# Re-ordered attention queues in a layer with split-precision matmuls: two score banks, three projection banks, work moved between VectorE, ACT and POOL

## The reference

```
x = x + attention(layernorm(x)) @ wo.T
    q, k, v = projections of layernorm(x); q = rope(q); k = rope(k)
    o[i] = sum over j <= i of exp(-slope_h * (i - j)) * (q[i] . k[j]) * v[j]
x = x + (fwht(silu(n @ W1.T) * (n @ W3.T))) @ W2.T      with n = layernorm(x)
```

## Time and profile before

| | us |
|---|---|
| median of 3 runs (range) | 283.77 (283.72 to 285.06) |
| the profiled execution | 284.03 |
| its span, first to last instruction | 282.2 |
| busy: PE / PEld / DVE / ACT / POOL | 260.7 / 225.8 / 222.1 / 162.2 / 132.6 |
| granted TensorE clock, mean | 1.000 |
| chain that ended last | PE 47%, DVE 37%, issue 7%, ACT 3%, DMA 2%, POOL 2% |

### The profile page before, as it was taken

One profiled execution on the slowest core, in us unless ns is written; L12 is line 12 of the kernel. 1 busy time (PEld: TensorE's weight loads), 2 busy tenths in 40 slices (PEclk: granted clock), 3 DMA queues, 4 the chain that ended last, 5 costly groups with the idle time before them and its releaser, 6 DMA issues.

```text
span 282.2 us, 4149 instructions
## 1 busy us (share of the span) xinstructions
PE 260.7 (92%) x1480; PEld 225.8 (80%) x1480; DVE 222.1 (79%) x340; ACT 162.2 (57%) x271; POOL 132.6 (47%) x101
## 2 busy tenths in 40 slices
PE   0798988999998899999999999889999999999995
PEld 0585877888786688878888888779889889988895
DVE  2878899999999998868999999999657795234323
ACT  1776877769377667655759657593643463033330
POOL 1049858477655746713584783478806500000000
PEclk9999999999999999999999999999999999999999
DMA  6694020220202110000001002200000000100002
GB/s 242 250 352 177 0 78 1 77 74 0 74 2 74 26 52 1 2 1 0 0 11 66 0 2 74 74 3 0 0 3 0 0 2 0 45 32 0 2 0 74
DMA packets 5203, 13.23 MB, mean 47 GB/s; under 512 B 576, under 2 KB 2112, under 8 KB 5184
## 3 DMA queue, kind: packets, MB, share of 16 engines
q1 hardware_dynamic: 4752, 12.65, 12.7%
q10 hardware_dynamic: 432, 0.33, 0.4%
HBM read 11.93 MB, written 1.05 MB: 46 GB/s over the span
## 4 chain that ended last, share of the span: by engine, by line
PE 47%; DVE 37%; issue 7%; ACT 3%; DMA 2%; POOL 2%; ACTq 0%; DVEq 0%
PE bank L263 16%; PE bank L264 15%; PE bank L265 15%; DVE rope_b L742 9%; DVE rope_a L741 6%; DVE bank L755 6%; DVE w_lo L716 5%; DVE o_lo L765 4%; DVE p_lo L760 4%; DMA sin_sb<-in_sin 2%; DVE xn L710 2%; PE bank L276 1%; POOL qk L625 1%; ACT o_hi L507 1%; DVE stats L693 1%
## 5 line engine op out<-in xcount | busy, mean ns | idle before, releaser
L625 POOL TENSOR_TENSOR qk<-rope_a,rope_b 128x512 f32<-128x512 f32 x40 | 52.1, 1304 | 54.8 <-DVE rope_b L742 54.8
L263 PE MATMUL bank<-xt_hi,w_hi 128*128 128x512 f32 x144 | 58.4, 405 | 3.4 <-DVE rope_a L741 2.3
L264 PE MATMUL bank<-xt_lo,w_hi 128*128 128x512 f32 x144 | 57.2, 397 | 0.0
L265 PE MATMUL bank<-xt_hi,w_lo 128*128 128x512 f32 x144 | 57.1, 396 | 0.0
L632 POOL TENSOR_TENSOR q_hid<-qk,q_hid 128x512 fp32r<-128x512 f32 x32 | 49.3, 1543 | 16.4 <-ACT q_hid L496 16.4
L503 ACT ACTIVATE p_hi<-bank 128x512 fp32r<-128x512 f32 x48 | 28.6, 597 | 40.5 <-DVE bank L755 40.1
L742 DVE TENSOR_TENSOR rope_b<-rope_b,sin_sb 128x512 f32<-128x512 f32 x40 | 43.3, 1083 | 0.0
L263 PEld LDWEIGHTS bank<-xt_hi,w_hi 128*128 128x128 f32 x144 | 27.6, 192 | 11.8 <-DVE rope_a L741 3.9
L265 PE MATMUL bank<-w_hi,o_lo 128*128 128x256 f32 x128 | 36.2, 283 | 0.0
L264 PE MATMUL bank<-w_lo,o_hi 128*128 128x256 f32 x128 | 36.2, 283 | 0.0
L263 PE MATMUL bank<-w_hi,o_hi 128*128 128x256 f32 x128 | 36.1, 282 | 0.0
(11 more groups left out here) (69 smaller groups left out, 574.0 us busy)
## 6 DMA issues: line engine op xcount, KB each, us to landing
w_raw<-in_w SPq DMA_DIRECT2D x6, 512.0 KB, 3.3
w_raw<-in_wq SPq DMA_DIRECT2D x4, 512.0 KB, 4.8
decay_sb<-in_decay SPq DMA_DIRECT2D x4, 512.0 KB, 5.6
w_raw<-in_wo SPq DMA_DIRECT2D x4, 512.0 KB, 3.3
x_sb<-in_x SPq DMA_DIRECT2D x4, 256.0 KB, 4.1
out<-x_sb SPq DMA_DIRECT2D x8, 128.0 KB, 1.8
w_raw<-in_wk SPq DMA_DIRECT2D x1, 512.0 KB, 5.7
w_raw<-in_wv SPq DMA_DIRECT2D x1, 512.0 KB, 7.4
```

The lines of the kernel that those rows point to most:

```text
L263: pe.matmul(o, a_hi, b_hi, start=first, stop=False, skip_group_check=shared)
L264: pe.matmul(o, a_hi, b_lo, start=False, stop=False, skip_group_check=shared)
L265: return pe.matmul(o, a_lo, b_hi, start=False, stop=last, skip_group_check=shared)
L625: pool.tensor_tensor(qk[:, r % 2, :], rope_a[:, r % 2, :], rope_b[:, r % 2, :], ALU.add).then_inc(rope_sum, 1)
```

## The change

- Projections use three banks in turn after the first eight tiles, scores two (banks 3 and 4): tile n = 3u + s takes bank n mod 2 and waits for the low part of tile n - 2. `p_hi` and `p_lo` get a second slot for `S_SECOND`, and ACT's `high_p` no longer waits for attention.
- PE's order in a unit: the key and the first query of unit u + 2 come before `S_FIRST1`, the second query behind it (before: both queries behind it and the key at the end).
- The orders of ACT, POOL and VectorE are rewritten to match. In unit 0 they are written out.
- The low parts of chunks 4 to 13 are written by POOL, those of 0 to 3 stay on VectorE; every wait for a chunk's low part names the engine's own semaphore through `wait_low_weights` (the SP loads, `project`, `project_values`, `project_out`, `up`). Chunk 3's parts come later, and chunk 4 is worked with the first ones (`FIRST_CHUNKS` 5), so each later chunk of the first half moves up by one unit.
- The norm of the halves prepared in units 0 to 5 and 8 to 13 is applied by ACT in unit 4 (12) as scale x + shift, with the shift computed by VectorE in unit 3 (11). The first half's and the feed-forward's last one stay on VectorE.

```diff
...
-FIRST_CHUNKS = 4
+FIRST_CHUNKS = 5
+LOW_ON_DVE = 4
...
-LIN = START + [i for u in range(UNITS) for i in values(u)[:2] + queries(u) + values(u)[2:] + key(u) + turned(u)]
+def projected(u):
+    return values(u)[:2] + key(u) + queries(u) + values(u)[2:] + turned(u)
+LIN = START + [i for u in range(UNITS) for i in projected(u)]
...
-FIRST_ROPE = 5
...
+LIN_BANKS, S_BANKS = 3, 2
+def p_slot(u, s):
+    return S_SECOND + 2 * (u % 2) if s == S_SECOND else s
...
-        p_hi = sb("p_hi", [P, 3, TOK], F32R)
-        p_lo = sb("p_lo", [P, 3, TOK], F32R)
+        p_hi = sb("p_hi", [P, 4, TOK], F32R)
+        p_lo = sb("p_lo", [P, 4, TOK], F32R)
...
+        shift = sb("shift", [P, TT])
...
-        s_bank = bank[2:5]
+        s_bank = bank[LIN_BANKS:LIN_BANKS + S_BANKS]
...
+        def wait_low_weights(engine, n):
+            if n < LOW_ON_DVE:
+                engine.wait_ge(w_lo_dve, n + 1)
+            else:
+                engine.wait_ge(w_lo_pool, n + 1 - LOW_ON_DVE)
...
-            return bank[n] if n < len(bank) else bank[n % 2]
+            return bank[n] if n < len(bank) else bank[(n - len(bank)) % LIN_BANKS]
+        def score_bank(u, s):
+            return s_bank[(3 * u + s) % S_BANKS]
...
                 if n >= len(bank):
-                    pe.wait_ge(lin_free, (n - 2 if n >= len(bank) + 2 else n - len(bank)) + 1)
+                    pe.wait_ge(lin_free, (n - LIN_BANKS if n >= len(bank) + LIN_BANKS else n - len(bank)) + 1)
                 return lin_bank(n)
...
-                if u:
-                    pe.wait_ge(p_lo_done, 3 * (u - 1) + s + 1)
+                n, o = 3 * u + s, score_bank(u, s)
+                if n >= S_BANKS:
+                    pe.wait_ge(p_lo_done, n - S_BANKS + 1)
...
-                        last = product(s_bank[s][:, b * 256:(b + 1) * 256], k_hi[:, ks, a], k_lo[:, ks, a],
+                        last = product(o[:, b * 256:(b + 1) * 256], k_hi[:, ks, a], k_lo[:, ks, a],
...
-                    last = product(s_bank[s][:], k_hi[:, ks, a], k_lo[:, ks, a],
+                    last = product(o[:], k_hi[:, ks, a], k_lo[:, ks, a],
...
                 if u < UNITS:
-                    fill(values(u)[:1])
+                    fill(values(u)[:2] + key(u) + queries(u)[:1])
                     scores(u, S_FIRST1)
-                    fill(values(u)[1:2] + queries(u))
+                    fill(queries(u)[1:] + values(u)[2:])
                 if u:
...
                 if u < UNITS:
-                    fill(values(u)[2:3])
                     attend(u, 0)
-                    fill(values(u)[3:] + key(u) + turned(u))
+                    fill(turned(u))
             up(0, 3)
...
+            def norm_apply(i, tiles):
+                half = i % HALVES
+                act.wait_ge(shift_done, i)
+                act.wait_ge(lin_full, LIN_NO[("X", i - 1, KD - 1)] + 1)
+                for t in tiles:
+                    act.activation(xn[:, t, :], x_sb[:, half * TT + t, :], ACT.Identity, bias=shift[:, t:t + 1],
+                                   scale=rstd[:, t:t + 1]).then_inc(xn_done, 1)
...
                 act.wait_ge(mask_done, n + 1)
-                if u:
-                    act.wait_ge(o_full, 2 * u - (s == S_FIRST0))
-                act.activation(p_hi[:, s, :], s_bank[s][:], ACT.Copy).then_inc(p_hi_done, 1)
+                act.activation(p_hi[:, p_slot(u, s), :], score_bank(u, s)[:], ACT.Copy).then_inc(p_hi_done, 1)
...
             high_weights(2)
-            high_weights(3)
             swap(("K", 0, 0))
             swap(("Q", 0, 0))
+            high_rope(("K", 0, 0))
             high_v(0, 0)
-            high_rope(("K", 0, 0))
             swap(("Q", 0, 1))
+            high_rope(("Q", 0, 0))
             high_v(0, 1)
-            high_rope(("Q", 0, 0))
             swap(("Q", 0, 2))
...
             high_v(0, 3)
+            high_weights(3)
+            high_weights(4)
+            high_p(0, S_FIRST0)
             high_rope(("Q", 0, 2))
-            high_p(0, S_FIRST0)
+            high_p(0, S_SECOND)
+            swap(("K", 0, 1))
+            high_p(0, S_FIRST1)
             high_rope(("Q", 0, 3))
-            high_p(0, S_SECOND)
-            for u in range(UNITS):
-                if u:
-                    before = queries(u - 1)
-                    fill(key(u - 1) + turned(u - 1))
-                    for item in before[:1]:
-                        high_rope(item)
-                    high_p(u, S_FIRST0)
-                    for item in before[1:]:
-                        high_rope(item)
-                    high_o(u - 1, 1)
-                    high_p(u, S_SECOND)
-                fill(values(u)[:2] + queries(u)[:1])
-                for item in key(u - 1) if u else []:
+            swap(("Q", 0, 4))
+            high_o(0, 0)
+            high_rope(("K", 0, 1))
+            swap(("Q", 0, 5))
+            high_rope(("Q", 0, 4))
+            high_weights(5)
+            for u in range(1, UNITS):
+                k, q, v = key(u), queries(u), values(u)
+                fill(turned(u - 1))
+                high_p(u, S_FIRST0)
+                for item in queries(u - 1)[1:]:
                     high_rope(item)
-                fill(queries(u)[1:])
+                high_p(u, S_SECOND)
+                high_o(u - 1, 1)
+                fill(v[:2] + k + q[:1])
                 high_p(u, S_FIRST1)
+                for item in k:
+                    high_rope(item)
+                fill(q[1:])
+                for item in q[:1]:
+                    high_rope(item)
+                fill(v[2:])
                 if u in (UNITS - 2, UNITS - 1):
                     silu(u - UNITS + 2)
-                fill(values(u)[2:3])
                 high_o(u, 0)
-                fill(values(u)[3:])
                 if unit_chunk(u) is not None:
                     high_weights(unit_chunk(u))
+                if u % PAIRS == 4:
+                    norm_apply(u // PAIRS + 1, range(TT))
             high_hid(0)
...
+            def low_weights(n):
+                _, _, at = CHUNKS[n]
+                pool.wait_ge(w_hi_done, n + 1)
+                pool.tensor_tensor(w_lo[:, at:at + CH], w_raw[:, n % SLOTS, :], w_hi[:, at:at + CH].bitcast(F32),
+                                   ALU.subtract).then_inc(w_lo_pool, 1)
...
             rope_add(("Q", 0, 2))
+            low_weights(4)
             rope_add(("Q", 0, 3))
...
             low_rope(("Q", 0, 3))
-            for u in range(UNITS):
-                if u:
-                    before = queries(u - 1)
-                    for item in before[:1]:
-                        low_rope(item)
-                    if u % PAIRS == 3:
-                        inverse_deviation(u // PAIRS + 1)
-                    for item in key(u - 1):
-                        rope_add(item)
-                    for item in before[1:] + key(u - 1):
-                        low_rope(item)
-                for item in queries(u):
+            rope_add(("K", 0, 1))
+            rope_add(("Q", 0, 4))
+            low_rope(("K", 0, 1))
+            low_rope(("Q", 0, 4))
+            rope_add(("Q", 0, 5))
+            low_weights(5)
+            for u in range(1, UNITS):
+                k, q = key(u), queries(u)
+                for item in queries(u - 1)[1:]:
+                    low_rope(item)
+                if u % PAIRS == 3:
+                    inverse_deviation(u // PAIRS + 1)
+                for item in k + q[:1]:
                     rope_add(item)
+                for item in k + q[:1]:
+                    low_rope(item)
+                for item in q[1:]:
+                    rope_add(item)
+                if unit_chunk(u) is not None:
+                    low_weights(unit_chunk(u))
                 if u >= UNITS - 2:
...
+            def norm_shift(i):
+                dve.wait_ge(rstd_done, i + 1)
+                if i == 2:
+                    dve.wait_ge(xn_done, TT * i)
+                dve.scalar_tensor_tensor(shift[:], mean_var[:, :, 0], -1.0, rstd[:], ALU.mult,
+                                         ALU.mult).then_inc(shift_done, 1)
...
             dve.wait_ge(tables_loaded, 48)
-            fill(START[2:5])
+            fill(START[2:10])
+            mask(0, S_FIRST0)
             low_weights(3)
-            fill(START[5:])
-            mask(0, S_FIRST0)
+            low_p(0, S_FIRST0)
             mask(0, S_SECOND)
-            low_p(0, S_FIRST0)
+            mask(0, S_FIRST1)
+            fill(START[10:] + key(0))
             low_p(0, S_SECOND)
-            for u in range(UNITS):
-                if u:
-                    mask(u, S_FIRST0)
-                    mask(u, S_SECOND)
-                    fill(key(u - 1) + turned(u - 1))
-                    low_p(u, S_FIRST0)
-                    low_o(u - 1, 1)
-                    low_p(u, S_SECOND)
-                fill(values(u)[:1])
-                mask(u, S_FIRST1)
+            fill(queries(0)[:1])
+            low_o(0, 0)
+            low_p(0, S_FIRST1)
```

(24 more changed lines are left out.)

27 lines of the change are left out of this document (15 added, 12 removed).

## The result

The changed kernel took 282.72 us in the median (279.93 to 283.67), the one before 283.91 beside it: ratio 0.9941, 95% interval 0.9920 to 0.9963. It is faster by 1.2 us (medians) to 1.7 us (ratio), where I had forecast 5.8. The profiled execution took 282.23 us, its span 280.4. Three of the 19 runs of the changed kernel had a mean granted clock of 1.000 and took 279.93, 280.51 and 280.80 us; the other 16, the profiled one among them, had 0.988 to 0.994 and took 282.23 to 283.67.

What follows compares the result with a forecast made beforehand. VectorE's queue, which TensorE waits for, was taken as the bound. Waits of 15.4 us would fall to 9.7 (6.5 of it entry): 284.03 - (15.4 - 9.7) = 278.3, as median 278.0; range 275.5 to 281.5, chance 0.45.

Steps and rivals of the forecast that it cites:

- VectorE's queue is the limit in the units with a chunk: Units 2 to 5, 12 and 13: TensorE waits mostly for VectorE's queue; waits in all units sum to 15.4 us.
- Chunk on POOL 2.5: Each of ten later chunks' low parts, a subtraction of 1024 columns, takes POOL 2.5 us.
- norm on ACT 1.8: Four activations of 256 columns in each half, before unit 5's and 13's first score copy: 1.8 us in all.
- The port's tax on VectorE: VectorE and POOL take turns reading SBUF; VectorE's sine product takes 0.67 us at best, 1.18 in the median.
- rivals B: POOL becomes the bound, unit 6 starts at 98.0 instead of 93.74: slower, 288 us, chance 0.18.
- a POOL turn: Unit 0: chunk 3's low part, behind the first mask and one POOL operation, ends at 29.9; first query waits 0.4.
- The entry, 6.5: Scores' start and units 0 and 1 lose 0.8 + 3.2 + 2.5 = 6.5 us, against 3.65 before; bounds 3 and 8.
- the 1.2 for unit 0's second tile: Unit 0: attention, ready at 34.95, waits for the second tile's low part until 36.1: 1.2 us.
- Units 2 to 14, 3.2: Small waits after the entry, from 0.95 us in unit 2 to 0.2 in units 14 and 15.
- my 8.5: Longest loop after the entry: 8.5 us plus port waits and hand-over, against TensorE's 9.77 in a unit without key.
- The bank waits go: Three projection banks remove waits of 1.19 us before unit 0, 1.15 at 87.69 and the like in unit 13.
- Rival C: Nothing gained: VectorE waits at the port what it sheds, the entry eats the banks' win: 283 us, chance 0.18.

Runs made afterwards that it cites:

- e14: Kernel before, with only the low parts of chunks from the fifth on moved to POOL and the later halves' norm on ACT: 276.99 us.
- e6: Changed kernel with the norm of units 3 and 4 (11 and 12) back on VectorE: 293.14 us.
- e4: Changed kernel plus 12 needless matmuls between unit 0's key and first query, keeping TensorE busy: 281.29 us.
- e8: Changed kernel with VectorE's variance and epsilon moved to the middle of units 3 and 11, the power behind two POOL sums: 282.90 us.
- e7: e3 with two projection and three score banks, as in the kernel before: 281.96 us.
- e3: e1, plus VectorE freeing the last value's bank and writing the second tile's low part before the third mask: 280.11 us.
- e5: Changed kernel with all chunks' low parts on VectorE: 297.58 us.
- e1: Changed kernel with chunk 3's high part (ACT) and low part (VectorE) back at their earlier places: 280.13 us.
- e2: Changed kernel with POOL's low part of chunk 4 moved behind the fourth query's: 282.08 us.
- e11: Changed kernel with another order of the entry on ACT and VectorE, POOL's order unchanged: 281.64 us.

## Why the prediction was wrong

The direction was right, the size was not: 1.2 to 1.7 us for 5.8. By its own steps ("the port" is the prediction's word for SBUF access, at which VectorE and POOL take turns):

- **VectorE's queue is the limit in the units with a chunk: right.** The two moves off VectorE win 6.7 by themselves (e14).
- **Chunk on POOL 2.5, norm on ACT 1.8: right**, measured 2.41 in the median and 2.07 for four; no table load stands beside them. The estimates from the Trainium skill's figures (GPSIMD Engine Reference, 3.1; ScalarE: Activation LUTs, What ACT_TABLE_LOAD costs) had been 2.25 and 2.3, 0.16 under and 0.23 over what was measured. The 2.3 had left out the 93 ns by which, as the Trainium skill states in the same section (ScalarE: Activation LUTs, What ACT_TABLE_LOAD costs), activations in a row overlap: with three overlaps the estimate is 2.07, as measured.
- **The port's tax on VectorE: right in kind, missed in size both ways.** The sine product's median fell from 1175 to 682 ns, so rivals B and C did not come true by it. But the tax is the rest of a POOL operation for each VectorE instruction that meets one, however short: 3.19 for a 1.22 split beside the chunk, 4.45 for three norm tiles in e6, 1.17 for four columns. I had charged "a POOL turn" at the split and ended it at 29.9; the turn was that of the chunk, and it ended at 31.17.
- **The entry, 6.5: the step that failed.** The scores started at 25.69 (forecast 26.8; 0.8 of it is that TensorE's first instruction came at 7.67 and not 8.48). Unit 0 took 13.41 for my 10.4: its first query waited 2.5, not 0.4 (1.3 of these 2.1 is the split's later end, the rest the scores' earlier start), and the clock fell behind it, an estimated 1.4 (e4), a term that the sum put at nothing without a reason. Unit 1 took 11.52 for 10.8. The waits in unit 1 were where I had put them (1.62 and 1.03 for 1.4 and 0.8), as was v_hid's (1.38 for 1.5); the 1.2 for unit 0's second tile came out at 0.15.
- **Units 2 to 14, 3.2: 5.0.** Units 2, 4, 5 and 6 came out at 0.26, 0.02, 0.32 and 0.09 for 0.95, 0.35, 0.45 and 0.05, which speaks for a loop shorter than my 8.5 and waits, though no run measured it. But units 3 and 11 lost 1.89 and 1.32 for 0.85 and 0.2, mostly by the variance step (e8), with the epsilon's addition in it: an instruction of four columns that I had not counted as a wait. Unit 14's lost 0.64 lies in the bounds of the 0.2.
- **Together:** unit 0 +3.0, unit 1 +0.7, units 2 to 14 +1.8, the scores' start -1.1, after unit 15's start -0.3: 4.1, where 282.23 - 278.3 = 3.9 is to be explained.
- **The bank waits go: right, and little is left of it.** The 1.04 for v_hid ahead of unit 0 went, and with the changed start the scores come 1.1 us sooner after TensorE's first instruction. Between the two profiled executions the changed kernel starts its scores 1.4 sooner than e14, loses 6.6 more in units 0 and 1 (9.37 for 2.81) and 0.4 more in units 2 to 14 (4.96 for 4.54), and wins 0.3 after unit 15's start: 5.3, and they differ by 5.3 (the medians by 5.7). The steady part was as good in the old order, once VectorE was relieved. In the new order the third projection bank still brings 1.9 (e7 against e3).

Rival C named the time (283), and half of its reason: the entry eats what is won. The other half, that VectorE waits away what it sheds, is refuted by its busy time (222.1 to 200.7).

Open: the key's place was not tried alone, neither undone in the changed kernel nor, with the old banks, done on the kernel before. Nor is it shown how e5's 14.9 and e6's 10.4 us divide between waits and clock. And what separates the runs at a clock of 1.000 from the others is not shown, since of no kernel were both kinds traced: in the changed kernel, e1 and e3 they were the faster ones, in e2 (282.28 and 282.54 for 281.83 and 281.88) and e11 they were not.

## What to carry to other kernels

When a change has several parts, cost each alone on the old kernel: here two small moves between engines were worth 6.7 us and the large re-ordering around them -5.7. Try also the pairs, for parts can need each other: the banks cost 31 us in the old order and bring 1.9 in the new one. Where several queues wait for each other, a stall at the entry moves from queue to queue (e2, e3, e11), so follow where a wait that went has gone before you count it as won. And put no long POOL operation beside a VectorE instruction that TensorE waits for soon.

## What the hardware showed

- In these traces a VectorE product, subtraction or scalar operation on SBUF alone that meets a POOL operation on SBUF tensors is held to that operation's end, whatever its own length: a tile of 0.40 took 2.45 beside a chunk of 2.41, and four columns took 1.17 for 0.17 at best. With POOL busy without a pause the engines take turns one for one (three tiles in 4.45 for 1.2 of work). It goes both ways: a POOL sum of 1.3 took 2.28. VectorE's subtractions that read PSUM were never stretched, nor were its norm statistics, though they read SBUF (ns, both of the changed kernel):

```profile
L823 DVE TENSOR_TENSOR p_lo<-bank,p_hi x48: 672/690/694, 31.1 to 204.7; 128x512 fp32r<-128x512 f32 x48
L748 DVE BATCH_NORM_STATS2 stats<-x_sb x16: 402/410/428, 3.7 to 222.3; 128x6 f32<-128x256 f32 x16
```

- After 2.5 us of waiting in unit 0 the granted clock went from 1.00 to 0.52, less than 1 us after work had gone on; with TensorE kept busy (e4) it did not. The estimated price of 1.4 us came on top of the wait itself. It is not sure to come: 2.86 us of waiting in e11 left the clock at 1.00.
- Undoing one part in the tuned order cost 15 and 10 us, where doing the same part alone in the old order brought 2.9 and 2.6. Here the price of an operation depended on its place more than on its length.
